# A causal attention block and a routed MLP in split float32: later groups of the input, and two tiles' probabilities, go through DRAM and are turned on VectorE instead of TensorE

## The reference

```
xn = layernorm(x) * gamma + beta
q, k, v = xn @ Wq, xn @ Wk, xn @ Wv
a = softmax(causal(q @ k.T / sqrt(512))) @ v          # within a batch
x1 = layernorm(x + (a @ Wo + x))
h = silu(silu(x1 @ w1.T) @ w3.T) @ w2.T
gates = the two largest of softmax(x1 @ wr.T), made to sum to 1
out = zeros; out[index of each chosen expert] += gate * h   # rows 0 to 7 alone
result = layernorm(x1 + out)
```

## Time and profile before

| what | value |
| --- | --- |
| time, median of 3 runs | 1635.58 us (1634.55 to 1635.96) |
| the profiled execution's own time | 1635.72 us |
| its span, first to last instruction | 1633.9 us |
| TensorE busy | 1615.7 us of it, 99% |
| VectorE, ScalarE, GpSimd busy | 885.7, 681.0, 283.8 us |
| granted TensorE clock | 1.00 throughout |
| moved by DMA | 136.64 MB in 365766 packets, 317008 of them under 512 B |

### The profile page before, as it was taken

How to read it: one execution, slowest core, us unless ns; L and a number is a source line. 1 busy time by engine, 2 the same in 40 slices (tenths; PEclk the granted TensorE clock), 3 DMA queues, 4 the chain that set the end, 5 groups by cost and what they waited for, 6 DMA issues and landing times.

```text
span 1633.9 us, 23601 instructions
## 1 busy us (share of the span) xinstructions
PE 1615.7 (99%) x7591; PEld 1335.6 (82%) x7591; DVE 885.7 (54%) x2296; ACT 681.0 (42%) x1301; POOL 283.8 (17%) x491
## 2 busy tenths in 40 slices
PE   9999999999999999999999999999999999999998
PEld 7888888888888888888888888888878888888886
DVE  5564645565364555455455545545565656556563
ACT  5443433353343344343333434343344444444442
POOL 1120201121120112121101212010131221212211
PEclk9999999999999999999999999999999999999999
DMA  4111625321154432123535123253664313223100
GB/s 161 59 61 52 155 76 139 100 94 56 60 136 104 113 94 95 54 91 107 134 85 123 61 76 104 78 138 97 157 133 63 51 26 51 37 40 51 26 0 8
DMA packets 365766, 136.64 MB, mean 84 GB/s; under 512 B 317008, under 2 KB 321104, under 8 KB 365664
## 3 DMA queue, kind: packets, MB, share of 16 engines
q1 hardware_dynamic: 354768, 116.48, 28.5%
q10 hardware_dynamic: 10896, 18.90, 3.6%
HBM read 79.73 MB, written 55.59 MB: 83 GB/s over the span
## 4 chain that ended last, share of the span: by engine, by line
PE 80%; issue 10%; DVE 4%; ACT 2%; POOL 2%; DMA 1%; ACTq 0%; POOLq 0%; SPq 0%; DVEq 0%
PE psum L351 25%; PE psum L353 25%; PE psum L352 25%; PE psum L1326 1%; PE psum L1262 1%; PE psum L1437 1%; PE psum L1436 1%; POOL rstd L512 1%; PE psum L1445 1%; PE psum L1444 1%; DVE pt_lo L934 1%; ACT affine L625 1%; ACT tok L641 0%; DMA raw<-in_wk_t 0%; DVE xt_hi L915 0%
## 5 line engine op out<-in xcount | busy, mean ns | idle before, releaser
L351 PE MATMUL psum<-xt_hi,g_hi 128*128 128x512 f32 (+3 forms) x640 | 237.5, 371 | 0.4 <-DVE g_lo L923 0.4
L353 PE MATMUL psum<-xt_lo,g_hi 128*128 128x512 f32 (+3 forms) x640 | 229.6, 359 | 0.0
L352 PE MATMUL psum<-xt_hi,g_lo 128*128 128x512 f32 (+3 forms) x640 | 229.3, 358 | 0.0
L351 PE MATMUL psum<-v_hi,pt_hi 128*128 128x512 f32 x544 | 220.8, 406 | 6.2 <-DVE pt_lo L934 3.9
L353 PE MATMUL psum<-v_lo,pt_hi 128*128 128x512 f32 x544 | 212.8, 391 | 0.0
L352 PE MATMUL psum<-v_hi,pt_lo 128*128 128x512 f32 x544 | 212.7, 391 | 0.0
L509 POOL TENSOR_TENSOR var_eps<-meanvar,eps 128x2 f32<-128x2 f32 (+1 forms) x97 | 18.9, 195 | 1005.4 <-DVE meanvar L901 1004.3
L946 DVE TENSOR_REDUCE rowmax<-psum 128x1 f32<-128x512 f32 (+3 forms) x160 | 97.1, 608 | 149.1 <-PE psum L353 147.7
L820 ACT ACTIVATE act_f<-psum 128x512 f32<-128x512 f32 x128 | 76.7, 599 | 199.7 <-PE psum L353 199.1
L641 ACT ACTIVATE tok<-tok,shift,rstd 128x512 f32<-128x512 f32 x128 | 97.5, 809 | 104.1 <-POOL shift L514 103.8
L590 POOL TENSOR_TENSOR expo<-euler,shifted 128x32 f32<-128x32 f32 x16 | 86.9, 5429 | 282.1 <-DVE shifted L1163 282.1
(11 more groups left out here) (149 smaller groups left out, 3400.6 us busy)
## 6 DMA issues: line engine op xcount, KB each, us to landing
xin<-in_x ACTq DMA_DIRECT2D x64, 256.0 KB, 2.8
tok<-in_x SPq DMA_DIRECT2D x64, 256.0 KB, 2.7
x_scratch<-tok SPq DMA_DIRECT2D x64, 256.0 KB, 2.2
out_dram<-tok SPq DMA_DIRECT2D x64, 256.0 KB, 2.3
p_scratch<-probs SPq DMA_DIRECT2D x64, 256.0 KB, 2.0
probs<-p_scratch SPq DMA_DIRECT2D x256, 64.0 KB, 2.5
x_in<-x_scratch SPq DMA_DIRECT2D x64, 256.0 KB, 4.3
p_scratch<-probs SPq DMA_DIRECT2D x16, 192.0 KB, 1.9
```

Source lines behind the costliest of these rows:

```text
L351: pe.matmul(o, ws, ms, start=first, stop=False, skip_group_check=True)
L352: pe.matmul(o, w_lo, ms, start=False, stop=False, skip_group_check=True)
L353: return pe.matmul(o, ws, m_lo_, start=False, stop=last, skip_group_check=True)
```

## The change

Only the first batch's groups 0, 1 and 2 and every batch's group 0 are still turned by TensorE. The others (group 3 of the first batch, groups 1, 2 and 3 of the rest) go another way: a normalised pair is stored from `xin` to a new DRAM buffer `xn_scratch`; a whole group is loaded back with 32x32 blocks exchanged, in 16 transfers of 64 KB (`load_xq`); VectorE turns inside the blocks (`turn_xq`); ScalarE applies gamma and beta (`affine_x`); VectorE rounds and subtracts (`split_xq`). The unrounded buffers `xt_a` and `xt_b` lie in the same memory as `xt_hi` and `xt_lo`, in the group's own columns. This work is one group ahead: group 1 in tile 15 of the batch before, group 2 in the projections after tile 2, group 3 in those after tile 6. Pairs are normalised in another order (2, 3, 4, 0, 1, 5, 6, 7), and SP issues their loads and stores, except for pairs 1 and 5 and those at the start. In the first batch pairs 6 and 7 are loaded at the start, into unused columns.

The probabilities of tiles 3 and 7 (`IN_WINDOW`) are stored and loaded by SP as those of far tiles are, and turned, rounded and subtracted in the projections ahead of their tile.

The diff, cut to its core:

```diff
-    FAR = range(2 * GROUP, TILES - 1)
+    FAR = [(t, c) for t in range(TILES) for c in range(chunks(t)) if (t in (GROUP - 1, 2 * GROUP - 1) or 2 * GROUP <= t < TILES - 1)]
+    xn_scratch = nc.dram_tensor("xn_scratch", [B * S, D], F32, kind="Internal").ap()
...
+        EARLY = (6, 7)
+        FIRST_ORDER = (0, 1, 2, 3, 6, 7, 4, 5)
+        ORDER = (2, 3, 4, 0, 1, 5, 6, 7)
+        FIRST_PE_GROUPS = 3
+        def in_dram(first, g):
+            return g >= (FIRST_PE_GROUPS if first else 1)
...
+        def pair_at(b, t, first, last):
+            if first:
+                pair = {0: 3, 1: 6, 2: 7, 3: 4, 4: 5}.get(t)
+                return None if pair is None else (b, pair, True)
+            if t < PEELED:
+                pair = {1: 6, 3: 7}.get(t)
+                return None if pair is None else (b, pair, False)
+            pair = {7: 2, 8: 3, 10: 4, 12: 0}.get(t)
+            return None if pair is None or last else (b + 1, pair, False)
@@ SP @@
+            def store_xn(b, pair, first=False):
+                sp.wait_ge(x_normed, normed_before(b, pair, first) + 1)
+                sp.dma_start(pair_rows(xn_scratch, b, pair), x_pair(pair, first)).then_inc(xn_stored, DMA)
+            def next_pair(b, pair, behind):
+                sp.wait_ge(xn_stored, stored_with(b, behind) * DMA)
+                load_pair(sp, b, pair)
+            def load_xq(b, g):
+                rows_of = xn_scratch[bass.ds(b * S + g * (GROUP * P), GROUP * P), :].rearrange("(t j) (c q i) -> q j c t i", j=LANES, q=QUADRANTS, i=LANES)
+                for c in range(DC):
+                    for q in range(QUADRANTS):
+                        sp.dma_start(xt_b[q * LANES:(q + 1) * LANES, c, columns(g)].rearrange("j (t i) -> j t i", i=LANES),
+                                     rows_of[q][:, c]).then_inc(xq_loaded[g], DMA)
             def tile(b, t, before=True, last=False):
                 sp.wait_ge(out_stored[slot], 1 + (b * USES + t // SLOTS) * DMA)
                 sp.dma_start(tok[:, slot, :], x[bass.ds(b * S + t * P, P), :]).then_inc(res_loaded[slot], DMA)
+                if t < PEELED and before:
+                    if t == 0:
+                        store_xn(b, 5)
+                    if t == 1:
+                        next_pair(b, 6, behind=5)
+                        load_xq(b, 2)
+                    if t == 3:
+                        next_pair(b, 7, behind=6)
+                    if t == 5:
+                        store_xn(b, 7)
...
+                if t >= PEELED and not last:
+                    if t == 7:
+                        load_pair(sp, b + 1, 2)
+                    if t == 9:
+                        next_pair(b + 1, 3, behind=2)
+                    if t == 11:
+                        next_pair(b + 1, 4, behind=3)
+                    if t == 12:
+                        store_xn(b + 1, 4)
+                    if t == TILES - 1:
+                        sp.wait_ge(scores_ready, b * CHUNKS + CHUNKS)
+                        load_xq(b + 1, 1)
...
+                if t == 2 and before:
+                    store_xn(b, 6)
+                if t == 5:
+                    sp.wait_ge(xn_stored, stored_with(b, 7) * DMA)
+                    load_xq(b, 3)
...
+                if not last:
+                    if t == 8:
+                        store_xn(b + 1, 2)
+                    if t == 10:
+                        store_xn(b + 1, 3)
+                    if t == 12:
+                        next_pair(b + 1, 0, behind=4)
@@ ScalarE @@
+            def affine_x(b, g, c):
+                act.wait_ge(xq_turned, dram_groups_before(b, g) * DC + c + 1)
+                act.activation(xt_b[:, c, columns(g)], xt_a[:, c, columns(g)],
+                               ACT.Identity, bias=beta_sb[:, c:c + 1], scale=gamma_sb[:, c:c + 1]).then_inc(affine_ready, 1)
...
                 if more and k == 2:
                     project_v(b, GROUP * (g + 1))
+                    if g + 2 < GROUPS and in_dram(not before, g + 2):
+                        for part in range(DC):
+                            affine_x(b, g + 2, part)
                     project_g(b, g + 1)
+                    if t + 1 in IN_WINDOW:
+                        for c in range(chunks(t + 1)):
+                            turn_probs(b, t + 1, c)
@@ VectorE @@
+            def turn_xq(b, g, c):
+                dve.wait_ge(xq_loaded[g], (b + 1 if g == GROUPS - 1 else b) * (DC * LOADS))
+                dve.transpose(xt_a[:, c, columns(g)], xt_b[:, c, columns(g)]).then_inc(xq_turned, 1)
+            def split_xq(b, g, c):
+                n = (b * GROUPS + g) * XUNITS + c + 1
+                dve.wait_ge(affine_ready, 1 + n)
+                dve.tensor_copy(xt_hi[:, c, columns(g)], xt_b[:, c, columns(g)]).then_inc(xt_hi_ready, 1)
+                dve.wait_ge(xt_hi_ready, n)
+                dve.tensor_tensor(xt_lo[:, c, columns(g)], xt_b[:, c, columns(g)], xt_hi[:, c, columns(g)],
+                                  ALU.subtract).then_inc(xt_ready, 1)
...
                     split_v(b, GROUP * (g + 1))
+                    if g + 2 < GROUPS and in_dram(not before, g + 2):
+                        for part in range(DC):
+                            turn_xq(b, g + 2, part)
+                        for part in range(DC):
+                            split_xq(b, g + 2, part)
                     split_g(b, g + 1)
+                    window = range(chunks(t + 1)) if t + 1 in IN_WINDOW else ()
+                    for c in window:
+                        turn_probs(b, t + 1, c)
+                    split_v(b, GROUP * (g + 1) + 1)
+                    for c in window:
+                        split_probs(b, t + 1, c)
@@ TensorE @@
-                if t != TILES - 1:
+                if t != TILES - 1 and t not in IN_WINDOW:
                     turn_probs(b, t, 0)
-                if more and k == 0:
-                    turn_x(b, g + 1, 0)
+                on_pe = not before and not in_dram(True, g + 1)
+                if on_pe and k == 0:
+                    turn_x(b, g + 1, 0, first=True)
...
                 if more and k == 2:
+                    if in_dram(not before, g + 1):
+                        pe.wait_ge(xt_ready, 1 + (b * GROUPS + g + 2) * XUNITS)
                     project_v(b, GROUP * (g + 1))
```

More of the change, by code:

```diff
@@ L230, in attention_mlp @@
                 TURNS += [("v", t + 1 + j) for j in range(GROUP)]
-            if t not in FAR:
-                TURNS += [("p", t, c) for c in range(chunks(t))]
+            TURNS += [("p", t, c) for c in range(chunks(t)) if (t, c) not in FAR]
         def turn_use(t, c):
@@ L534, in tile @@
                 pool.tensor_tensor(y, y, y, ALU.add).then_inc(res_doubled, 1)
[L535 to L538, removed]
+                slot = pair_at(b, t, not before, last)
+                if slot and t in AT_MIDDLE:
+                    norm_x(*slot)
                 if t == TILES - 2 and not last:
@@ L559, in _ @@
             for pair in range(FIRST_PAIRS):
-                norm_x(0, pair)
+                norm_x(0, pair, first=True)
             for t in range(PEELED):
@@ L612, in fold_to_hi, with turn_x @@
                     act.activation((m_hi, wvo_hi)[pair][:, n % DC, :], psum[:, fold_bank(n), :], ACT.Copy).then_inc(fold_hi, 1)
[L614 to L622, removed]
+            def turn_x(b, g, u, first=False, then_load=None):
+                act.wait_ge(xt_ready, 1 + b * (GROUPS * XUNITS) + g * XUNITS + u)
+                act.wait_ge(x_turned, turned_before(b, g, u, first) + 1)
                 for k in range(2):
@@ L730, in tile @@
                     norm_behind(b, t - 2)
-                if more and k == 1:
-                    norm_x(b, 2 * (g + 1) + 1)
+                slot = pair_at(b, t - 1, not before, last) if t else None
+                if slot and t - 1 in AT_END:
+                    norm_x(*slot)
                 for c in range(max(chunks(t), n_next)):
@@ L735, in tile @@
                         turn_probs(b, t, c)
-                    if more and k == 2 and c == chunks(t) - 1:
-                        turn_x(b, g + 1, 3, more=not (last and g + 2 == GROUPS))
+                    if on_pe and k == 2 and c == chunks(t) - 1:
+                        turn_x(b, g + 1, 3, first=True, then_load=2 * (g + 2) if g + 2 < FIRST_PE_GROUPS else None)
                     if c < n_next:
@@ L994, in tile @@
                     chunk_max(b, t + 1, c)
-                if t != TILES - 1:
+                if t != TILES - 1 and t not in IN_WINDOW:
                     split_probs(b, t, 0)
-                if t in FAR:
+                if (t, 1) in FAR and t not in IN_WINDOW:
                     turn_probs(b, t, 1)
-                if more and k == 0:
+                on_pe = not before and not in_dram(True, g + 1)
+                slot = pair_at(b, t, not before, last)
+                if on_pe and k == 0:
                     split_x(b, g + 1, 0)
@@ L1039, in tile @@
                     norm_behind(b, t - 1)
```

(8 more changed lines are left out.)

247 lines of the change are left out of this document (156 added, 91 removed).

## The result

The changed kernel takes 1646.33 us (median of five runs, 1644.34 to 1649.43), the kernel before beside it 1635.96 us (1634.55 to 1636.86): a ratio of 1.0063, 95% interval 1.0050 to 1.0075. It is slower by 0.6%, where 1632 was forecast. The profiled execution is the slowest of the five, 1649.43 us with a span of 1647.6, and TensorE's mean granted clock in it is 0.990 (0.990 to 0.996 over the five; 1.0 in the profile before).

What follows compares the result with a forecast made beforehand. TensorE, busy 1615.7 of 1633.9 us, was taken as the bound: 1635.7 - 22.4 (work leaving) + 16.2 (tile 2's waits) + 3.0 (tile 4's) = 1632.5 us, predicted as 1632; range 1614 to 1644, likeliest case 1626 to 1639.

Steps and rivals of the forecast that it cites:

- the sum: Whole kernel: 1635.7 - 22.4 + 16.2 + 3.0 = 1632.5 us; 1626.2 and 1638.2 by the bounds of the load.
- the cases: Four outcomes: tile 2 wait with clock held 0.42, wait hidden 0.25, clock falls 0.20, SP's far tiles 0.13.
- the list of what would make the prediction wrong: No gap in tile 2, 0.43 us pitches behind it, waits in tiles 9 to 13, new waits in tile 15.
- The likeliest case: TensorE waits in tile 2 of later batches with its clock held: predicted 1632 us, range 1626 to 1639, chance 0.42.
- it fell: TensorE's clock halves in tile 2's three waits, 1.9 us more each: 1638.2 us, chance 0.20.
- The third rival: SP's queue in tiles 8 to 12 delays probabilities, up to 3.7 us per tile: 1647.5 us, chance 0.13.
- What leaves TensorE: 160 turns of x and 48 of probabilities, 52 units at 0.44 us, less 0.5: 22.4 us saved.
- changeover: On TensorE, 0.08 us lost per unit in changing over to the next product, beside 0.36 for its four turns.
- the small waits of tile 1: TensorE's waits in tile 1 of later batches, said to be gone after the change; no size given.
- The wait in tile 2: Before tile 2's attention in three later batches, 16 x loads delay a store: 5.4 us each, 16.2 in all.
- Tile 4: Before tile 4's attention in three later batches, x units no longer cover the low half: 1.0 us each, 3.0 in all.
- Moved work at nothing: Turns and splits moved to VectorE fit its slack in projections and tile 15, cost nothing; without cover, 36 us of VectorE.

Runs made afterwards that it cites:

- the edit: Tile 9's next pair of x loads moved behind its stores of probabilities: 1645.5 us on the changed kernel alone; 1619.6 with two other edits, 1625.0 without it.
- the run with the head at 728: Changed kernel with 18 warming matmul calls at the start for 14: 1638.5 us, ratio 1.0010 to the kernel before.

## Why the prediction was wrong

**The step that failed is the sum: it had no term for TensorE's own code.** It counted the instructions that leave TensorE, and not that four of them stood ahead of the loop, so that its head moved from 724 to 720. The pauses at the loop's return cost 10.8 us in the profile. A head moved to 716 costs the kernel before 7.4 us with nothing else changed (5.7 of them at the return), and moving it from 720 to 728 gains 8.2, 9.8 and 10.2 us. None of the cases had a place for it, nor did the list of what would make the prediction wrong. That the place of the head sets it is shown by these four pairs of runs. That the pause is the fetching of code behind the branch's target is argued and not shown: it has no releaser, only instruction queues move, and it keeps to one place in the code. The Trainium skill says (page "Runtime: NRT & Kernel Launch", section "Instruction fetch mechanics") that a taken branch to code outside the fetched pages must wait for a transfer. The trace agrees for the branch itself, 3.3 to 3.8 us in the two kernels and mostly hidden by queued matmuls; the second pause, 2.8 to 3.5 us of the sequencer, is not in that rule.

**The likeliest case had the clock held, and it fell.** The prediction gave that 0.20. The trace shows 1.2 GHz behind tile 2 in all three batches, at 2.0 us each (1.4 to 2.3) against the 1.9 taken from the program's start. Filling the wait with 36 calls holds the clock in all three, and with 18 the time falls by 5 to 6 us. What the page "TensorE: Matmul & The Clock Gate" of the Trainium skill says in Part 1, that an idle array goes back to half its clock, is what these rows show. I chose against it because the only long idle stretch of the old trace was its end, where there was no later work to see a slow pace in.

**The third rival was right in mechanism, and smaller.** A store and a wait in front of the probabilities made them late, in tile 9 alone and in three batches: 7.6 us in the profile, 5.0 as the edit's worth, against 15 for its six waits of 2.5. It had the load of these tiles too high: tiles 8 to 11 have three chunks, so 12 loads of 0.67 us and not 16. The time fell into its range, above 1644, but by luck: the larger part of the miss is the loop's return.

**What leaves TensorE was under-sized.** The forecast was 22.4 us; 28.6 came off (19.1 and 9.5). The unit's own 0.36 us is exact (19.1 over 52 is 0.37). Behind it the sum had 0.08 of changeover, and in fact 0.18 went with each unit: the prediction named the small waits of tile 1 that would go, and gave them no term, and 1.2 us are three waits of 0.4 ahead of tile 4's second chunk, which go because the first chunk now waits. For tiles 3 and 7 alone, 12 units at 0.44 make 5.3, and 5.6 was measured.

**The wait in tile 2 was right, place and chain.** Against the batch's start, SP's residual load was forecast at 642.2 and came at 642.2; the loads began 0.2 us after the forecast; the store came at 652.7 for 654.9. The term that was off is the load's issue: 0.55 us (16 from 654.10 to 662.95), 0.55 to 0.58 over the three batches, where the lower bound was 0.57 (the upper one should have been 0.67 + 0.18 = 0.85). So the wait is 12.1 us in all and not 16.2. The 0.18 for an address from the loop's register is not seen: ahead of the loop, where the address is a constant, 16 such loads take as long (8.8 us from 115.30). **Tile 4** was right: 2.8 us of waiting for 3.0.

**Moved work at nothing** held in the changed kernel only because TensorE came late to the projections. With tile 2 mended, VectorE's turns and splits hold it up for 3.7 us.

So 1632.5 becomes, by the terms of the profiled execution: 6.2 less for what leaves, 4.1 less for tile 2's wait, then 6.0 more for its clock, 10.8 for the loop, 7.6 for tile 9, 0.5 for tile 4 and 2.4 for the first 30 us. That is 1649.5, against 1649.43. Without the loop's term it is 1638.7, and the run with the head at 728 took 1638.5, inside the forecast's own range, in part by luck: its other terms are off by 10.3 us one way and 16.5 the other.

Two things stay open: why the first 30 us lose 2.4 (TensorE waits 1.3 us for low halves of weights there, and x of two more pairs is loaded at that time), and which places of a loop's head are good ones, since only four were tried, within 12 matmuls.

## What to carry to other kernels

Instructions removed ahead of a loop move the loop's head, and at 1640 us that can cost more than the instructions did; if a gap stands at the loop's return with "issue" as its releaser, a few idle instructions ahead of the loop are the cheapest experiment there is. Before a queue gets a new piece of work, list which store behind it some engine waits for: both waits of this change were stores behind loads that nobody needed yet, and the same loads one place later, with the head moved on, turn a loss of 0.6% into a gain of 1%. And an idle stretch of TensorE is to be priced with the slow pace that follows it.

## What the runs showed of the hardware

- A branch back on TensorE takes 3.3 to 3.9 us of its sequencer in the runs here, mostly hidden behind the queued matmuls, and a second pause behind its target depends on where the target stands. With 724 or 728 matmuls ahead of the loop there is none, and TensorE idles for at most 0.8 us; with 720 the pause is 2.8 to 3.5 us and TensorE idles for 2.9 to 4.1; with 716 it is 2.8, and TensorE idles for 1.9.
- A matmul of the identity by itself in float32 (the warming call) stands as two matmuls in the traces; a turn against the identity stands as one.
- In the changed kernel the granted clock fell to 1.2 GHz behind each of the five idle stretches of 2.9 to 4.3 us, and behind one of the four of 1.7 to 1.9.
- Sixteen DMA issues of 64 KB, each with an address that walks three dimensions, leave SP's queue every 0.55 to 0.58 us in the changed kernel, as fast from the loop's register as from a constant; those of the probabilities take 0.67.
